# Prefetch hints on the loops over sequences and over expert pairs, and an earlier gather for an expert's sixth group

## What is computed

```python
probs = softmax(x @ gate_w); w, sel = top_k(probs, 8); w = w / sum(w)
# per expert: up to C = 2048 slots, filled in the order of the tokens
xg = x_pad[t_slot].reshape(E, C, H)                    # E = 32, H = 512
g, u = xg @ w_gate, xg @ w_up                          # H -> 192
y = (silu(g) * u) @ w_down                             # 192 -> H
out.at[t_slot].add(w_slot * y)
```

## Time and profile before

| | us |
|---|---|
| median of 3 runs | 2829.18 |
| lowest and highest | 2825.65, 2830.83 |
| the profiled execution | 2820.11 |
| its span, first to last instruction | 2818.3 |

### The profile page before, as it was taken

The page is one execution under the profiler, slowest core; times in us unless marked ns, Lnnn a source line. Parts: engine busy times, 40 slices in busy tenths (PEclk is TensorE's granted clock), DMA queues, the critical chain, the costliest instruction groups (busy, mean ns, idle before and its releaser), DMA issues. The chain is left out here.

```text
span 2818.3 us, 60760 instructions
## 1 busy us (share of the span) xinstructions
PE 2340.0 (83%) x19991; PEld 1654.9 (59%) x19992; DVE 1718.5 (61%) x3264; ACT 1123.9 (40%) x2753; POOL 1466.4 (52%) x1699
## 2 busy tenths in 40 slices
PE   0788888888888888888872799899999999998994
PEld 0565665656665665666652466566666666665673
DVE  3576766767667676776742456466565566664662
ACT  0234334343434434334341344344444444443441
POOL 3134444545445454454544666566666666665673
PEclk9999999999999999999995799899999999999997
DMA  5000000000000000000000777687787787876787
GB/s 120 16 28 19 26 22 26 26 19 26 22 26 27 19 26 19 26 26 23 23 16 31 155 159 164 124 166 168 154 167 176 138 166 164 168 160 130 158 162 180
DMA packets 159545, 244.44 MB, mean 87 GB/s; under 512 B 43952, under 2 KB 77744, under 8 KB 159280
## 3 DMA queue, kind: packets, MB, share of 16 engines
q0 software_dynamic: 74752, 155.51, 29.4%
q1 hardware_dynamic: 80048, 79.21, 9.5%
q10 hardware_dynamic: 4608, 8.39, 0.8%
HBM read 144.72 MB, written 106.69 MB: 89 GB/s over the span
## 5 line engine op out<-in xcount | busy, mean ns | idle before, releaser
L1666 POOL DMA_INDIRECT acc_scratch<-y,m_add x300 | 482.7, 1609 | 367.0 <-POOLq L1673 306.6
L1791 PE MATMUL ps<-xh,wh 128*128 128x256 f16 x1752 | 420.3, 282 | 58.6 <-PEq L1803 58.5
L1792 PE MATMUL ps<-xh,wl 128*128 128x256 f16 x1752 | 420.1, 282 | 0.0
L1658 POOL DMA_INDIRECT xg<-z_scratch,slot_t x292 | 295.6, 1012 | 89.5 <-issue 75.0
L582 POOL DMA_INDIRECT slot_scratch<-pair,slots x256 | 259.2, 1013 | 79.8 <-issue 79.0
L1868 ACT ACTIVATE y<-ps,wts_now 128x512 f32<-128x512 f32 x294 | 186.1, 684 | 218.1 <-ACTq L1867 218.1
L1796 PE MATMUL ps<-xl,wh 128*128 128x256 f16 x1752 | 243.5, 276 | 4.1 <-PEq L1807 4.1
L899 PEld LDWEIGHTS ps<-xnT,wqk 128*128 128x128 f32 x2048 | 235.1, 193 | 16.6 <-issue 16.6
L1791 PEld LDWEIGHTS ps<-xh,wh 128*128 128x128 f16 x1752 | 177.1, 101 | 109.0 <-issue 72.0
L899 PE MATMUL ps<-xnT,wqk 128*128 128x128 f32 x2048 | 235.3, 276 | 1.4 <-PEq L1070 1.4
L1942 DVE SCALAR_TENSOR_TENSOR hx<-ps,s 64x256 f16<-64x256 f32 x146 | 62.1, 426 | 269.4 <-DVEq L1964 269.0
(11 more groups left out here) (273 smaller groups left out, 5054.7 us busy)
## 6 DMA issues: line engine op xcount, KB each, us to landing
wst<-in_L_ffn_w_gate_dram SPq DMA_DIRECT2D x32, 384.0 KB
wst<-in_L_ffn_w_up_dram SPq DMA_DIRECT2D x32, 384.0 KB
xt<-in_x_dram SPq DMA_DIRECT2D x32, 256.0 KB, 2.6
ct<-in_ctx_dram SPq DMA_DIRECT2D x32, 256.0 KB, 2.6
acc_scratch<-x SPq DMA_DIRECT2D x32, 256.0 KB, 2.0
z_scratch<-zn ACTq DMA_DIRECT2D x32, 256.0 KB
wdst<-in_L_ffn_w_down_dram SPq DMA_DIRECT2D x32, 256.0 KB
acc_scratch<-y,m_add POOLq DMA_INDIRECT x300, 5.1
```

The source lines that it names most:

```text
L1658: pool.indirect_dma_start(out=xg[b][:, h, :], out_offset=None, in_=z_d[:, :], in_offset=bass.IndirectOffsetOnAxis(ap=rows(h), axis=0)).the ...
L1666: pool.indirect_dma_start(out=acc_d[:, :], out_offset=bass.IndirectOffsetOnAxis(ap=m_add[:, k, h:h + 1], axis=0), in_=y[:, k, h, :], in_of ...
L1791: pe.matmul(ps[:, dst, 0:GROUP], wh[:, j, k, c0:c0 + P], xh[:, k, :], start=(k == 0), stop=False)
L1792: pe.matmul(ps[:, dst, 0:GROUP], wl[:, j, k, c0:c0 + P], xh[:, k, :], start=False, stop=False)
```

## The change

In `written_out_groups` the sixth group is written out in front of the loop, which is left with the seventh and eighth and now uses buffer 3. On POOL the sixth group's gather goes into the If of the fourth group, in front of `add_rows(y_buffer(3))`; its `add_rows` joins the loop of those of the fifth. Gathers of the seventh and eighth go to buffer 3.

```diff
@@ first part, POOL; the same on ACT, PE and DVE
-                with pool.Fori(4, nb) as j:
+                with nc.Fori(4, nb, engines=[pool.engine], hint_back_edge=True) as j:
                     step(j)
@@ pairs_of_experts
-                with eng.Fori(0, ne // 2 - 1) as i:
+                with nc.Fori(0, ne // 2 - 1, engines=[eng.engine], hint_back_edge=True) as i:
@@ written_out_groups
                 with eng.If(n > USUAL * GROUP):
-                    with eng.Fori(USUAL, NGRP) as g:
+                    group(USUAL, 2)
+                    with eng.Fori(USUAL + 1, NGRP) as g:
                         with eng.If(n > g * GROUP):
-                            group(g, 2)
+                            group(g, 3)
@@ expert, on POOL
-                    for g in range(3, USUAL):
+                    with pool.If(n > 3 * GROUP):
+                        with pool.If(n > USUAL * GROUP):
+                            gather_group(e, USUAL, 2)
+                        add_rows(y_buffer(3))
+                    for g in range(4, USUAL + 1):
                         with pool.If(n > g * GROUP):
                             add_rows(y_buffer(g))
-                    for g in range(USUAL, NGRP):
+                    for g in range(USUAL + 1, NGRP):
                         with pool.If(n > g * GROUP):
-                            gather_group(e, g, 2)
+                            gather_group(e, g, 3)
                             add_rows(y_buffer(g))
```

More of the change, by code:

```diff
@@ L857, in _ @@
                 step(3, pairs=False)
-                with act.Fori(4, nb) as j:
+                with nc.Fori(4, nb, engines=[act.engine], hint_back_edge=True) as j:
                     step(j)
@@ L1136, in _ @@
                 step(3, pairs=False)
-                with pe.Fori(4, nb) as j:
+                with nc.Fori(4, nb, engines=[pe.engine], hint_back_edge=True) as j:
                     step(j)
@@ L1513, in _ @@
                 step(3, pairs=False)
-                with dve.Fori(4, nb) as j:
+                with nc.Fori(4, nb, engines=[dve.engine], hint_back_edge=True) as j:
                     step(j)
```

## The result

| us | before | after |
|---|---|---|
| median | 2827.41 | 2709.74 |
| lowest and highest of 4 runs | 2823.31, 2830.83 | 2708.53, 2713.55 |
| the profiled execution | 2820.11 | 2708.53 |
| its span | 2818.3 | 2706.7 |

The ratio is 0.9587, with an interval of 0.957 to 0.9604: 4.1% faster. The direction was right, and the size was missed by 113 us. In size this is rival B, "the hint works in full on DVE and PE", at 2713, to which the prediction gave a chance of 0.20.

What follows compares the result with a forecast made beforehand. PE was taken as the bound, delayed by DVE's code fetches at its closing branch and late sixth-group gathers. Terms -28 + 1.5 - 10 + 29 + 1 = -6.5 took the median from 2829.2 to 2823 us, range 2712 to 2848.

Steps and rivals of the forecast that it cites:

- rival B: Loop over pairs: hint brings the head's block and the next back in time on DVE and PE; 2713 us, chance 0.20.
- What bounds the kernel: PE's loop over pairs: 14 groups at DVE's closing branch cost 90.7 us too much, three sixth groups 28.3.
- The gather, -28: POOL's sixth-group gather, moved ahead of a scatter, lands before PE needs it; -28 us, bounds 20 to 28.3 saved.
- The sequences, +1.5: Hints in the four loops over sequences: one more instruction per engine and round, nothing to prefetch; +1.5 us, bounds 0 to 8.4.
- (a): DVE's closing branch, loop over pairs: hinted fetch starts some 0.5 us earlier; -10 us, bounds 0 to 90.7 gained.
- (b): DVE's loop over pairs: new instructions move a code-block boundary before L1954, delaying PE's gate_up signal; +29 us, bounds 0 to +49.
- (c): PE's loop over pairs: its longer body may outgrow its buffer, the stall running beside DVE's; 0 us, up to 6.48 per round otherwise.
- The rule of the purely sequential prefetch: Loop over pairs: a loop's head is never brought back in time, which speaks against any gain from (a).
- E, the slower side: Loop over pairs: block boundary before L1954 costs its full +49 us and 10 us of (a) don't come; 2852 to 2860, chance 0.17.

Runs made afterwards that it cites:

- dve_pair_unhinted: Changed kernel with the hint taken off DVE's loop over pairs alone, all others kept; 2891.6 us, ratio 0.943 to the kernel before.
- end91_nohint: Changed kernel without the hint on DVE's loop over pairs, plus 91 semaphore increments on DVE ahead of that loop; 3051.49 us, ratio 0.9908.
- end91_hint: Changed kernel with 91 semaphore increments on DVE ahead of its loop over pairs, DVE's hint kept; 2992.23 us, ratio 0.9723.
- long_body_all: Changed kernel, hints kept, with some 90 never-executed instructions behind each written-out group of DVE, its body then 1028 instructions; 3091.44 us, ratio 1.0087.
- head_pad2: Kernel before, no hint, with two more semaphore increments on DVE ahead of its loop over pairs; 2848.02 us, ratio 1.0087.
- no_hints: Changed kernel with all five hints off, sixth group still written out and gathered early; 2860.95 us, ratio 1.0136 to the kernel before.
- gather_and_pad5: Kernel before with POOL's earlier sixth-group gather and five increments ahead of DVE's loop over pairs, no hint; 2966.99 us, ratio 0.9663; on another chip 0.9693.
- dve_hint_only: Kernel before with one edit, the hint on DVE's loop over pairs; 2736.07 us, ratio 0.9682.
- pair_hints_only: Changed kernel without the hints on the four loops over sequences; 2975.5 us, ratio 0.968; on further chips 0.9714 and 0.9711.
- head_pad5: Kernel before, no hint, with five more semaphore increments on DVE ahead of its loop over pairs; 2732.07 us, ratio 0.9676.

## Why the prediction was wrong, step by step

**What bounds the kernel: right.** The two kinds of group and their excesses, 90.7 and 28.3 us, are what the change took away (89.1 and 28.1). Reading 5.37 us of "waiting at L1950" as a fetch of code was right too: the run that has the same rows and waits, but five instructions ahead of the loop, doesn't have the gap.

**The gather, -28: right.** -28.1. POOL's timeline has the order that was described, the sixth group's gather at 1768.66, ahead of a scatter, 8.1 us before PE turns to the group at 1776.76:

```profile
1768.66 0.94 POOL L1659 DMA_INDIRECT xg<-z_scratch,slot_t  x1 [0.30 <-issue]
1769.91 0.94 POOL L1659 DMA_INDIRECT xg<-z_scratch,slot_t  x1 [0.30 <-issue]
1771.15 1.62 POOL L1667 DMA_INDIRECT acc_scratch<-y,m_add  x1 [0.30 <-issue]
```

**The sequences, +1.5: not refuted on the chip of the forecast, incomplete elsewhere.** The loop over pairs starts 4.3 us later, within 0 to 8.4, but kernels without these hints differ by as much among themselves there, so the term itself isn't measured. "A gain is excluded, since nothing is fetched" was too strong a sentence: on two of three other chips kernels with these hints are 66 to 80 us ahead by then, from a cause that stays open.

**(a), -10: this is the step that failed.** It asked how many microseconds earlier a fetch would start, 0.5, and never asked whether the fetch had to be there. The rows could have raised that question: the loop has 263 instructions and the code came in five packets a round, so a reader had to ask why a loop of four blocks is fetched whole every time. In the changed kernel the loop stays held and no packets of DVE's are left: 89.1 us go in place of 10, all but 0.1 of the 6.48 a round. Two things kept the loop there in the runs. One is its place: five idle instructions do it in the kernel before without any hint, and dve_pair_unhinted has 104.02 us in the 14 groups with DVE's hint off. The other goes with the hint, where the place is bad: 190.73 us in end91_nohint, 105.42 in end91_hint. So the prediction took the gain to depend on when the hint fetches, while in the changed kernel the place alone would have brought it. What throws a badly placed loop out, a fetch behind its end for instance, no run shows. The 0.5 us of the step is nearer to what goes with the hint where the loop isn't held, 1.2 us in long_body_all.

**(b), +29: the mechanism is real, its premise wasn't.** head_pad2, which moves the code by two instructions, costs 31.2 us in the 14 groups and 23 in the median. In the changed kernel there is no second stall, as there is no first one, and in dve_pair_unhinted there is neither, even without DVE's hint. The two terms (a) and (b) were added as if independent; they are one, since the second stall lives only where the first does.

**(c), 0: wrong in its size and right in its outcome.** The body did outgrow what PE holds, and "4 to 5 us that run beside DVE's stall" was a bad bound: PE stands 7.7 us a round in no_hints, and taking its hint away costs 152 us on the second chip, 10.8 in each of 14 rounds, more than the 6.48 of DVE's miss. The Trainium skill's limit (Runtime: NRT & Kernel Launch, Instruction fetch mechanics) of 2048 instructions for PE would have let 1641 fit; q8's 111 packets in no_hints disagree. With PE's hint the term is 0; whether another place of PE's code would do it too, as with DVE's, no run tries. Writing the sixth group out, which made PE's body that long, wasn't needed for the gather's 28 us: gather_and_pad5 leaves it in its loop and is as fast in the second part (1195 us against 1197).

**The rule of the purely sequential prefetch.** From what the same section of the Trainium skill says, that prefetch is purely sequential, the prediction drew that nothing could be gained in (a). The 14 groups at 104.97 us in dve_hint_only disagree with that conclusion. They don't show a fetch across the branch, since none of DVE's packets is left there: the gain comes without one.

**The rivals.** B's sum, 2713, was 3 us off, with a mechanism that the runs don't bear out: it has the head and the next block fetched in time, and 18 packets on q14 and one on q8 are all that is fetched in 956 us. Its number is right because a stall that is hidden and one that doesn't arise take away the same 90.7 us. It got 0.20 because "two instructions of notice" seemed to speak against it, which is only an argument if the hint acts by fetching. The range ended at B's sum without the bounds of B's own terms: the gather's 28.3, zero for the hints and the sequences at zero give 2710. E, the slower side, has its mechanism in head_pad2 (2848 us). no_hints, at 2861, is as slow as E said, but by PE's stall, which E didn't have.

**Sum.** As forecast, -28 + 1.5 - 10 + 29 + 1 = -6.5; as measured in the profiled executions, -28.1 + 4.3 - 89.1 + 0 + 1.3 = -111.6.

No version was faster than the changed kernel on a chip where both ran. gather_and_pad5, without any hint, is within the intervals of pair_hints_only on both chips where the two met (0.9663 and 0.968, 0.9693 and 0.9714), with a shorter program; where the sequence hints go with the shorter rounds, it is 69 us behind.

## What to carry to other kernels

An engine that stands still behind a loop's closing branch, with "waiting" for something that has long been there and packets on its code queue in each round, was fetching its loop again in these kernels. Ask first why the code isn't there any more, and only then how early it could come: here a hint, or a few instructions that moved the loop, took the whole stall and the half clock behind it. Test the two apart: a change that adds a hint also moves the code, and here the place alone was enough. Before writing more code out in a loop, count what each engine's body grows to, because the engine whose body is no longer held may be another one; here it was PE, and its stall cost more than DVE's.

## What the runs showed of the hardware

- A branch that is hinted and a loop that is held: 0.27 us from DVE's closing branch to its next instruction (4.7 before). Unhinted but well placed: 0.32 in head_pad5, 0.33 in dve_pair_unhinted. Unhinted and badly placed, by 91 idle instructions: 4.6.
- A hinted loop of 1028 instructions: 3.0 us, against 4.2 unhinted, with no difference in the second part's time.
- PE, whose body of 1410 instructions was held without a hint, is held at 1641 with one and not without in the two kernels that lack it; unheld, it stands 7.7 us and fetches some 8 packets of 16 KB a round (111 in 956 us, 1.82 MB).
- Two idle semaphore increments ahead of a loop made the kernel 0.9% slower, five made it 3.2% faster.
- The same first part takes 44.3 us a round on one chip and 47.7 or 51.2 on three others.
